# First-layer attention on one Trainium2 core: the two head pairs' denominators are broadcast together, and the numerators keep one PSUM bank

## What is computed

```python
h = relu(layernorm(x))                       # per node, 256 features
q, k, v = h@Wq.T+bq, h@Wk.T+bk, h@Wv.T+bv    # 4 heads of 64
scores = clip(q @ k_chunk.T / 8, -10, 10)    # keys in 8 chunks of 256
scores = where(adj == 0, -10, scores)
attn = softmax(scores, over the 256 keys of ONE chunk)
ctx = sum over chunks of attn @ v_chunk
out = layernorm(ctx @ Wo.T + bo + h) * gamma + beta
x = x + out
```

## Time and profile before

| | |
|---|---|
| median of 3 runs | 4598.11 us (4597.84 to 4601.86) |
| profiled execution | 4597.83 us, span 4596.0 us |
| TensorE busy (matmul) | 4386.1 us, 95% |
| VectorE, ScalarE, GpSimd busy | 76%, 65%, 65% |
| last scores of the first layer | begin at 2865.8 us |
| second layer begins | at 2922 us |

### The profile page before, as it was taken

How to read it: one execution, slowest core, us unless ns; L and a number is a source line. 1 busy time by engine, 2 the same in 40 slices (tenths; PEclk the granted TensorE clock), 3 DMA queues, 4 the chain that set the end, 5 groups by cost and what they waited for, 6 DMA issues and landing times. The chain is left out here.

```text
span 4596.0 us, 84237 instructions
## 1 busy us (share of the span) xinstructions
PE 4386.1 (95%) x34312; PEld 2615.8 (57%) x34312; DVE 3494.4 (76%) x4562; ACT 2987.9 (65%) x3498; POOL 3009.0 (65%) x2422
## 2 busy tenths in 40 slices
PE   7999999999999999999999999389999999999997
PEld 3334334334334334333333433279999999999997
DVE  5875775775776776776687577478898989889895
ACT  4664664664665565556466466188887888888885
POOL 5685685675775676577477477356665757667585
PEclk9999999999999999999999999689999999999999
DMA  6001000000001000001000000111121212112011
GB/s 197 10 10 37 10 10 28 19 10 28 19 10 28 19 10 28 10 10 33 15 10 19 10 10 19 35 47 50 56 68 41 75 32 70 54 47 82 29 59 42
DMA packets 126979, 160.88 MB, mean 35 GB/s; under 512 B 8832, under 2 KB 109184, under 8 KB 126592
## 3 DMA queue, kind: packets, MB, share of 16 engines
q1 hardware_dynamic: 126592, 155.49, 10.7%
HBM read 121.64 MB, written 33.83 MB: 34 GB/s over the span
## 5 line engine op out<-in xcount | busy, mean ns | idle before, releaser
L583 ACT ACTIVATE e_sb<-e_sb 128x1024 f32<-128x1024 f32 x1024 | 1082.4, 1058 | 835.7 <-DVE e_sb L684 798.3
L684 DVE SCALAR_TENSOR_TENSOR e_sb<-psS,mask 128x1024 f32<-128x1024 f32 x1024 | 1202.9, 1216 | 348.0 <-PE psS L815 341.5
L1414 PE MATMUL psA<-xy,ring_p 128*128 128x195 bf16 x8192 | 1405.1, 248 | 13.6 <-DVE red L1294 13.6
L1414 PE MATMUL psA<-xy,ring_s 128*128 128x195 bf16 x8192 | 1404.6, 249 | 0.0
L414 POOL TENSOR_TENSOR e_sum<-e_sb 128x1024 f32<-128x1024 f32 x384 | 918.5, 2392 | 325.5 <-ACT e_sb L583 219.0
L1214 ACT ACTIVATE ring_s<-eiB,ejb 128x1024 int8<-128x1024 f32 x1024 | 1089.8, 1137 | 9.5 <-PE psA L1414 9.5
L815 PE MATMUL psS<-qT,kT 64*128 64x512 f32 x4096 | 1042.2, 613 | 3.0 <-DVE e_sb L684 2.9
L828 PE MATMUL psN<-e_sb,v_sb 128*32 128x512 f32 x8192 | 985.0, 598 | 0.0
L1414 PEld LDWEIGHTS psA<-xy,ring_p 128*128 128x128 fp8e4 x8192 | 801.5, 98 | 19.9 <-DVE red L1294 17.0
L1414 PEld LDWEIGHTS psA<-xy,ring_s 128*128 128x128 fp8e4 x8192 | 800.5, 98 | 8.6 <-issue 0.3
L431 POOL TENSOR_TENSOR ctxT<-ctxT,num 128x512 f32<-128x512 f32 x384 | 488.1, 1277 | 456.2 <-DVE num L659 349.9
(11 more groups left out here) (120 smaller groups left out, 4158.0 us busy)
## 6 DMA issues: line engine op xcount, KB each, us to landing
eiB<-ei_between SPq DMA_DIRECT2D x64, 512.0 KB, 4.1
xin<-x SPq DMA_DIRECT2D x32, 512.0 KB, 3.9
xr<-x SPq DMA_DIRECT2D x32, 512.0 KB, 4.8
x_between<-hy SPq DMA_DIRECT2D x32, 512.0 KB, 3.2
xin<-x_between SPq DMA_DIRECT2D x32, 512.0 KB, 5.6
xo<-x_between SPq DMA_DIRECT2D x32, 512.0 KB, 4.5
out<-o_sb SPq DMA_DIRECT2D x32, 512.0 KB, 5.3
xr<-adjT SPq DMA_DIRECT2D x24, 512.0 KB, 4.1
```

Of the source, the lines that this page charges most:

```text
L583: act.activation(e_sb[:, n % ES], e_sb[:, n % ES], ACT.Exp, scale=SCALE).then_inc(exp_done, 1)
L684: dve.scalar_tensor_tensor(out=e_sb[:, n % ES], in0=psS[:, s % 2], scalar=-CLIP_RAW, in1=mask[:, kb, cols][:, None, :].to_broadcast([P, 2, ...
L1414: ins = pe.matmul(psA[:, i % BANKS, br * PARTS * XW:(br + 1) * PARTS * XW], part[:, n % RING, k, tt * TW + j * P:tt * TW + (j + 1) * P], x ...
```

## The change

- `psM` has two banks now, `psN` one. Both pairs' broadcasts of a chunk are issued one behind the other, each from its own 64 rows of the array and into its own bank, with one wait ahead and one signal behind them.
- They stand always behind the group's scores, at offsets 5, 6, 7 and 8.
- `normalize` and `add_to_ctx` handle a chunk of both pairs in one instruction (1024 elements a partition). `num` has 14 slots, so that a chunk's two slots lie side by side.
- `numerators` of group g wait for the copy of group g-1.
- In `project`, the second half's matmuls have a bank of their own and no longer wait for `y_done`.
- All transposes go into `psS[:, 0]`, and those of tiles 1 to 3 are moved from behind the K matmuls to the middle of the V matmuls; they wait for `q_done`.

```diff
-NS = 13
+NS = 14
-PICKS = ((5, 1), (6, 0), (6, 1), (7, 1), (8, 0), (8, 1), (9, 1), (10, 1))
+PICK_AT = (5, 6, 7, 8)
-        psN = ps("psN", [P, PAIRS, TW])
+        psN = ps("psN", [P, TW])
-        psM = ps("psM", [P, TW])
+        psM = ps("psM", [P, PAIRS, TW])
...
         def turned(t):
-            return psN if t else psS[:, 0]
+            return psS[:, 0]
         def turned_at(t):
-            return K_AT[t - 1] + 1 if t else 0
+            return K_AT[t - 1] + 3 if t else 0
...
+            def add_to_ctx(b, half, c):
+                chunk = half % 2 * CPH + c
+                if chunk == 0:
+                    return
...
+                    pool.tensor_tensor(ctxT[:, :, :], ctxT[:, :, :], slots(n), ALU.add).then_inc(ctx_done, 1)
...
+            def normalize(b, half, c):
+                n, h = b * GROUPS + half * GPH + c * PAIRS, b * HALVES + half
+                dve.wait_ge(bcast_done, h * CPH + c + 1)
+                dve.wait_ge(numcopy_done, n + PAIRS)
+                dve.tensor_tensor(slots(n), slots(n), psM[:, :, :], ALU.mult).then_inc(norm_done, 1)
...
             def turn(b, t, first):
-                if t == 1 and not first:
-                    pe.wait_ge(numcopy_done, b * GROUPS)
+                if t:
+                    pe.wait_ge(q_done, (b * T + t) * PAIRS)
...
-                        if t + 1 < T:
-                            turn(b, t + 1, first)
...
                     j = v - K_AT[t] - 2
+                    if j == 1 and t + 1 < T:
+                        turn(b, t + 1, first)
...
-                    if u % KPC == 0 and g >= PAIRS:
-                        pe.wait_ge(numcopy_done, b * GROUPS + g - 1)
+                    if u % KPC == 0 and n:
+                        pe.wait_ge(numcopy_done, b * GROUPS + g)
...
+                for pair in range(PAIRS):
+                    rows = slice(64 * pair, 64 * pair + 64)
+                    ins = pe.matmul(psM[:, pair, :], pick[rows, c * PAIRS + pair, :], r_s[rows, :], start=True, stop=True)
+                ins.then_inc(bcast_done, 1)
```

More of the change, by code:

```diff
@@ L235, in layer0 @@
         HALVES = 2 * T
-        CTX = T * (2 * GPH - PAIRS)
+        CTX = T * (CH - 1)
         def ctx_until(g):
-            i = g % (2 * GPH)
-            return g // (2 * GPH) * (2 * GPH - PAIRS) + (i + 1 if i < PAIRS else i + 1 - PAIRS)
+            chunk = g // PAIRS
+            return chunk // CH * (CH - 1) + max(chunk % CH, 1)
         SUMMED = GPH - PAIRS
@@ L268, in tile_at, with picked, slots @@
             return t - 1 if r == 0 and 1 <= t <= T else None
-        def picked(k, where):
-            return [(half_at(k, off), i) for i, (off, at) in enumerate(PICKS)
-                    if at == where and half_at(k, off) is not None]
+        def picked(k):
+            return [(half_at(k, off), c) for c, off in enumerate(PICK_AT) if half_at(k, off) is not None]
+        def slots(n):
+            first = n // PAIRS * PAIRS % NS
+            return num[:, first:first + PAIRS, :]
         def alive(b, k):
@@ L480, in _ @@
                     for bb, kk in alive(b, k):
-                        for where in range(2):
-                            for half, i in picked(kk - 1, where):
-                                add_to_ctx(bb, half * GPH + i)
+                        for half, c in picked(kk - 1):
+                            add_to_ctx(bb, half, c)
                     if 1 <= k <= GROUPS:
@@ L745, in _ @@
                     for bb, kk in alive(b, k):
-                        for half, i in picked(kk, 1):
-                            normalize(bb, half * GPH + i)
+                        for half, c in picked(kk):
+                            normalize(bb, half, c)
                         invert(bb, kk)
@@ L849, in denominators, with broadcast @@
                 ins.then_inc(sums_done, 1)
-            def broadcast(b, half, i):
+            def broadcast(b, half, c):
                 h = b * HALVES + half
-                if i == 0:
+                if c == 0:
                     pe.wait_ge(r_done, h + 1)
-                if i == 0 and h >= 2 and h % 2 == 0:
+                if c == 0 and h >= 2 and h % 2 == 0:
                     pe.wait_ge(y_done, h)
[L857 to L861, removed]
+                elif h or c:
+                    pe.wait_ge(norm_done, h * CPH + c)
+                for pair in range(PAIRS):
+                    rows = slice(64 * pair, 64 * pair + 64)
+                    ins = pe.matmul(psM[:, pair, :], pick[rows, c * PAIRS + pair, :], r_s[rows, :], start=True, stop=True)
+                ins.then_inc(bcast_done, 1)
             def project(b, k):
@@ L874, in project @@
                             for pair in range(PAIRS):
[L875 removed]
+                                ins = pe.matmul(psM[:, j, a * F:(a + 1) * F], ctxT[:, pair, col:col + P],
                                                 w_o[:, pair, :], start=pair == 0, stop=pair == PAIRS - 1)
@@ L895, in _ @@
                     for bb, kk in alive(b, k):
-                        for half, i in picked(kk, 1):
-                            broadcast(bb, half, i)
+                        for half, c in picked(kk):
+                            broadcast(bb, half, c)
                     if 1 <= k <= GROUPS:
```

37 lines of the change are left out of this document (10 added, 27 removed).

## The result

The changed kernel takes 4534.4 us (median of 4 runs, 4533.5 to 4534.6) against 4600.0 for the kernel before (4 runs): ratio 0.9857, 95% interval 0.984 to 0.9874. The profiled execution has a span of 4532.8 us, 63.2 less. The forecast was 4549, range 4533 to 4580.

A forecast was written before the change was run, and what follows sets the result against it. TensorE's own program was taken as the bound. Terms of -21.8 (groups), -41 (gap), +15 (one bank), +5 (GpSimd) and -6 (start and end) sum to -48.8: 4597.8 to 4549 us, range 4533 to 4580.

The forecast's parts named there:

- Pair for the price of one: Groups: a pair of broadcasts costs what one costs, saving the broadcasts at offsets 9 and 10; -21.8 us.
- The gap: Gap between elements: fewer normalization waits, broadcasts and copy waits, less some exposed transposes' copies; -5.8 a gap, -41 us.
- in the new order K and Q of tile 0 follow each other ... -1.3: Gap, tile 1's K matmuls: reordering with the transposes removes their wait for a late `v_sb` copy; -1.3 us a gap.
- One bank: Numerators wait for the previous group's copy: no stall in regular groups, stalls in groups 58 and 61; +15 us.
- The ring's 14th slot at 0: `num` ring: the extra slot ends 62 us of ScalarE waits that cost TensorE nothing; 0.
- GpSimd and VectorE: GpSimd's longer additions delay group 23's denominators, +5 us; VectorE's wider instructions stay ahead, 0.
- the case that I had named but not summed: Group 20: if VectorE's `r_s` operation loses to GpSimd's `b_o` addition, group 21's broadcast is 1.0 us late.
- The end: Bare chain at the very end: shorter additions, earlier second projection half and one wait fewer; -6 us.
- A: Rival: a pair's two broadcasts run serially, +56 us, giving 4605 us and no gain; chance 0.07.
- B: Rival: the bank wait stalls regular groups by 0.1 to 0.3 us, giving 4564 to 4594 us; chance 0.13.
- C: Rival: the gap gives nothing, as transposes' copies queue behind VectorE's normalizations; 4581 us; chance 0.06.
- D: Better than forecast: GpSimd's queue empties and `turn_h` costs half; 4528 to 4536 us; chance 0.1.

The follow-up runs named there:

- same_rows: Changed kernel with both broadcasts of a pair taken from array rows 0 to 63 instead of each from its own 64 rows; 4589.4 us.
- gap_wait: `narrow` plus, in the gap and behind the last group, the second broadcast of a chunk waiting for the first one's normalization; 4591.0 us.
- turns_moved: Kernel before with only the transposes changed: into the scores' banks and in the middle of the V matmuls; 4595.6 us.
- strict14: Kernel before, two numerators' banks kept, with numerators of group g waiting for the copy of g-1 and 14 ring slots instead of 13; 4611.6 us.
- narrow: Changed kernel with each chunk's normalization and ctx addition split into two instructions of 512 elements; 4538.0 us.
- hb_later: Changed kernel with the residual's two GpSimd additions 5 groups later (HB_AT 9 instead of 4); 4530.4 us.
- best: Changed kernel with next-input preparations ahead of the exponentials, GpSimd's rsqrt one group earlier, and residual and output work moved later; 4511.8 us.

## Why the prediction was right, and where it was off

- **Pair for the price of one**: right. Offsets 9 and 10 gave 21.9 us (21.8 forecast); the array rows that differ are the cause (`same_rows`).
- **The gap**: right in kind, 6.44 instead of 5.8 us. The waits for a normalization were 1.27 as counted (`gap_wait`: 1.32 each). The step "in the new order K and Q of tile 0 follow each other ... -1.3" had the right size and a wrong reason: not the transposes' new place removed the wait (0.36 alone, and `turns_moved` still waits), but the single broadcast whose normalization stood ahead of the reciprocals. The +0.2 for tile 3's copies did not come: its K follows V by 1.73 us, as in the tiles without a broadcast. And a dropped broadcast was worth 0.63, not 0.43, since it also lengthens what stands on either side of it: the transposes take 0.97 us ahead of one and 0.87 without, Q 3.54 behind one and 3.44 without. Two of them make the other 0.4 us.
- **One bank**: the two places and only these, as forecast (I had counted them as groups 58 and 61; the numerators in question stand behind the scores of 59 and 62); 13.5 us instead of 15. The mis-sized term is "0.25": a released wait costs 0.14 to 0.15. In the earlier trace rows the numerators did not wait for ScalarE. They stood behind a broadcast of group 1, which waited for its normalization. After the change that broadcast is gone, and group 1 takes 4.04 us. I had put broadcasts in groups 0 and 1 at nothing, "where TensorE waits for the first exponentials anyway"; they cost 0.23.
- **The ring's 14th slot at 0**: with two banks it is worth nothing as far as the runs show (all groups of `strict14` but 59 and 62 are as long as in the kernel before; the slot alone was not run), but that misleads; with one bank it is worth some 14 us.
- **GpSimd and VectorE**: +5 forecast and +3.6 measured, but that the size came out is partly luck. I had the +5 in group 23, whose denominators were to wait 0.6 to 0.9 us longer; they wait 0.41 less. What happened was the case that I had named but not summed: the operation on `r_s` loses by less than 0.1 us, group 21 takes 1.0 us more, and GpSimd's queue gains that time. In the one element of `narrow` in which VectorE won, group 23 took 7.04 us, 1.05 more than before, so the step that I had summed is right for the case that did not come. What I did not count is that groups 37 and 53 had the same collision before and lose 0.37 us of it. In 15 of the 16 places GpSimd's addition had a lead of 0.57 us in the kernel before and the operation on `r_s` took 2.35 us; now the lead is 0.96 and it takes 1.97. Both times it ends 0.55 us behind the addition. In `hb_later` and `best`, with no addition beside it, it takes 0.74. That is 6 us, the largest term missed.
- **The end**: -5.5 of -6, by other parts. The last half's broadcasts start 3.8 us sooner after the last scores, not 1.3: the operation on `r_s` starts 2.1 us sooner and takes 0.79 us instead of 2.49, for there too it had been held up by an addition. `gap_wait` has the waits back and loses 4.3 us here, with `r_s` at 2.25 us again. From the first of these broadcasts to the last addition 1.8 us are saved (2 forecast). The 1.3 for the projection's second half did not come: its output follows the first half's by 3.0 us, 2.8 before. It does start without waiting now, but its matmuls ran at a granted clock of 0.50 (the 1.2 GHz level, since 2822.7, after TensorE had stood idle; up again at 2843.2), where before the clock was back at 1.00 when they began. In `best`, where the clock rose in time for them, the second output follows by 1.8 us.
- **Rivals**: A is refuted by `same_rows`, B by the unmoved groups of 3.77 us (their copies are 0.40 to 0.48 us ahead of the numerators, of which 0.14 are needed), C by a gap of 56.5. D came true in its size but not in its reasons, and the result lies only 1.4 us inside the range.

Of the 15 us between forecast and result, groups 37 and 53 are 6, the gap 4.5, group 1, the one bank and group 23 with 21 another 4.5. All of them fell on the same side.

## What to carry to other kernels

When one engine's program is the bound, read its pace from the starts of rows and count per place, since the same broadcast cost 0.23, 0.01, 0.63 or 1.7 us depending on its neighbours. A matmul that uses half of the array's rows can be paired with one on the other half for next to nothing (0.008 us here). The bank for that may be taken from a buffer whose copy has slack; then look where long operations stand between the work and that copy. Before a cause is put to a wait, read what stands ahead of the waiting instruction on its own engine.

## What the runs showed of the hardware

- Two float32r matmuls of 64 rows on different rows run side by side: +0.008 us for the second, +0.225 if both use the same rows. With 128 rows after 64-row scores, the broadcast also starts 0.5 us later (1.92 after the scores' start instead of 1.42); among matmuls of 128 rows, in the gap, the 128-row pairs cost no more than the 64-row ones (56.50 us both).
- VectorE's operation with both inputs in SBUF (744 ns) took 2.88 us when a GpSimd addition had started 0.03 us ahead, and GpSimd's addition took 2.83 instead of 2.37 when VectorE had started first. The Trainium skill, SBUF — State Buffer, "Who interferes with whom", says that a VectorE instruction with two SBUF inputs contends with a GpSimd instruction that reads SBUF, and that issue order decides who blocks; these rows agree. Normalizations with one input in PSUM stayed at 1203 to 1222 ns.
- A 128x1024 normalization takes 1210 ns against 2 x 679, and an addition on GpSimd 2368 against 2 x 1277: one instruction saves 0.15 to 0.19 us.
